# First maxima row in one piece, second stack behind it, b's stores by part

## The reference, cut to what matters

```python
def reference(x, cond, ...):          # x (8, 256, 256), cond (8, 512), all float32
    # layer 0: modulated attention, 16 heads of 16 channels
    xs = layernorm(x * s1)
    q, k = (xs @ Wq.T) * q_dc, (xs @ Wk.T) * k_dc
    v = (xs @ Wv.T) * v_dc * s2
    p = softmax(q @ k.T * 0.25)
    x = x + (p @ v) @ Ww.T * w_dc + (v @ Wu.T) * u_dc
    # layer 1: gated state space, 512 channels, 16 states
    xr, gate = split(x @ W_in.T); xr = xr + cond
    xc = silu(conv4(xr)); xn = layernorm(xc) * g + b
    Bm, Cm, dt = split(xn @ W_xproj.T)
    Ad = 1 - 0.01 * tanh(dt @ W_dt.T + b_dt) * tanh(A_log)
    Bd = Bm * min(norm(xn), 1)
    for t in range(256):              # sequential
        h = clip(h * Ad[t] + Bd[t] x xn[t], -10, 10); y[t] = C[t] . h
    return x + (y + D * xn) * silu(gate) @ W_out.T
```

## Time and profile before

| | |
|---|---|
| median of 3 runs | 540.82 us |
| the profiled execution's own time | 541.88 us |
| its span | 539.0 us |
| TensorE / VectorE / ScalarE / POOL busy | 476.7 / 431.6 / 256.6 / 171.8 us |

### The profile page before, as it was taken

How to read it: one execution, slowest core, us unless ns; L and a number is a source line. 1 busy time by engine, 2 the same in 40 slices (tenths; PEclk the granted TensorE clock), 3 DMA queues, 4 the chain that set the end, 5 groups by cost and what they waited for, 6 DMA issues and landing times.

```text
span 539.0 us, 8625 instructions
## 1 busy us (share of the span) xinstructions
PE 476.7 (88%) x3064; PEld 288.4 (54%) x3084; DVE 431.6 (80%) x751; ACT 256.6 (48%) x512; POOL 171.8 (32%) x195
## 2 busy tenths in 40 slices
PE   6974998999999989888999887689998999999996
PEld 6842765767676656567898453133333333333333
DVE  6795355777857786849998986899999999999994
ACT  3442476767577646779686765343311111111111
POOL 5145303213031100000640100798783334333332
PEclk8695799999999999999999999999999999999999
DMA  8656374553645620100057547676546433333310
GB/s 311 243 176 169 137 176 100 156 142 97 156 99 148 149 77 1 41 19 21 2 198 242 185 150 168 220 265 199 158 136 135 143 116 117 107 104 104 105 36 22
DMA packets 45606, 71.81 MB, mean 133 GB/s; under 512 B 19097, under 2 KB 34073, under 8 KB 42892
## 3 DMA queue, kind: packets, MB, share of 16 engines
q1 hardware_dynamic: 37556, 64.66, 40.7%
q10 hardware_dynamic: 7480, 3.06, 2.3%
q0 software_dynamic: 528, 3.55, 1.7%
HBM read 41.88 MB, written 23.02 MB: 120 GB/s over the span
## 4 chain that ended last, share of the span: by engine, by line
PE 55%; DVE 27%; DMA 7%; ACT 5%; issue 3%; SPq 1%; POOL 1%; ACTq 1%; another core or an unknown queue 0%; DVEq 0%
DVE win L1926 9%; PE bank L1079 7%; PE bank L1537 6%; PE bank L1137 5%; PE bank L1497 5%; DVE z L1926 5%; PE bank L1508 5%; PE bank L1105 5%; PE bank L1122 4%; PE bank L1196 3%; PE bank L1174 3%; DVE acc L1715 3%; DVE lnb_rep L1926 3%; PE bank L1325 2%; DVE zlast L1926 2%
## 5 line engine op out<-in xcount | busy, mean ns | idle before, releaser
L1737 DVE TENSOR_REDUCE mx<-bank 128x2 f32<-128x512 f32 x128 | 82.0, 685 | 58.1 <-PE bank L1105 57.7
L1497 PE MATMUL bank<-xst,bst 128*128 128x512 bf16 x238 | 76.3, 383 | 22.2 <-DVE win L1926 8.9
L763 ACT ACTIVATE ex<-bank 128x512 f32<-128x512 f32 x128 | 70.8, 599 | 40.7 <-PE bank L1122 40.7
L1926 DVE CUSTOM_DVE_ANT_0 win<-win,bank,hi 128x512 f32<-128x512 f32 x96 | 71.8, 748 | 4.0 <-PE bank L1325 0.7
L1508 PE MATMUL bank<-win,cst 128*32 128x512 f32 x256 | 67.3, 605 | 0.2 <-DVE zlast L1926 0.2
L1497 PEld LDWEIGHTS bank<-xst,bst 128*128 128x128 bf16 x256 | 24.6, 97 | 70.4 <-DVE win L1926 27.4
L1105 PE MATMUL bank<-kst,qst 127*128 127x256 bf16 x256 | 48.6, 283 | 8.1 <-DVE mx L1737 7.2
L1122 PE MATMUL bank<-qst,kst 128*128 128x256 bf16 x256 | 46.5, 275 | 9.8 <-DMA qst<-mT 7.1
L1079 PE MATMUL bank<-xnT,w 128*128 128x256 f32 x192 | 49.2, 410 | 1.7 <-ACT xnT L663 0.9
L517 POOL TENSOR_TENSOR qk<-qk,part 128x512 f32<-128x512 f32 x14 | 16.2, 1156 | 101.3 <-ACT part L678 101.3
L621 POOL TENSOR_TENSOR yg<-yT,gateT 128x128 f32<-128x128 f32 x60 | 29.4, 523 | 56.7 <-ACT yT L1012 56.7
(11 more groups left out here) (218 smaller groups left out, 928.1 us busy)
## 6 DMA issues: line engine op xcount, KB each, us to landing
xs_d<-xpart SPq DMA_DIRECT2D x15, 384.0 KB, 4.8
xst<-xs_d SPq DMA_DIRECT2D x15, 384.0 KB
qk_d<-part SPq DMA_DIRECT2D x58, 96.0 KB, 2.4
xn_d<-xc SPq DMA_DIRECT2D x16, 256.0 KB, 4.0
xtk<-xn_d SPq DMA_DIRECT2D x64, 64.0 KB
xst<-xs_d SPq DMA_DIRECT2D x15, 256.0 KB
bd_d<-zeros POOLq DMA_DIRECT2D x1, 3468.0 KB, 13.1
qst<-qk_d SPq DMA_DIRECT2D x7, 384.0 KB, 3.9
```

The source lines that it names most:

```text
L763: nc.scalar.activation(ex[:, n // 4, n % 4, :], bank[6 + n % 2][:, :], ACT.Exp, scale=SCALE)\
L1497: mm(bank[t % 4][:, :], bst[:, slot, t % RS, :], xst[slot][:, t % RS, :], start=True, stop=True)\
L1737: v.tensor_reduce(mx[:, :, STACKED[n]:STACKED[n] + 1], bank[4 + n % 2][:, :].rearrange("p (t k) -> p t k", t=HALVES), AX.X, ALU.max)\
L1926: v._custom_dve(bass.dve_ops.TENSOR_ADD_SAT, out=zst[t % ZR], in0=zst[(t - 1) % ZR], in1=bank[t % 4][:, :], s0=hi[:, t:t + 1], s1=0.0).the ...
```

## The change

Sample 0's row of maxima is made in one piece, like the others: `turn_first_half` and `take_first_half` go, `scores(0, 0, 2)` and the exponentials of its heads move into `sample(0)`. SP stores its half of sample 1's stack, waits for `m_row`, and loads both q and k (six DMAs); ACT stores only. At the hand-over, `split` counts `bsplit` after each part; SP sends pairings 0 to 2 after the first part and 3 after the second, ahead of xn of tile 6; ACT sends x parts of tile 6 and the first rows of tile 7, then pairings 4 and 5. Gates are taken in order 5, 6 and `u_steps(0)` waits for seven. The `store_parts` helper takes the engine as an argument; where nothing else changes in such a line it is left out here.

```diff
@@ SP
                     sp.wait_ge(s["third_ready"], 2)
+                if b == 1:
+                    sp.wait_ge(s["m_row"], 16)
                 if b >= NBUF:
                     sp.wait_ge(s["st_done"], (b - NBUF + 1) * NH)
-                load_stack(sp, b, 0, NH, (f"ld_q{buf}", f"ld_k{buf}"), (0,) if b == 1 else (0, 1))
+                load_stack(sp, b, 0, NH, (f"ld_q{buf}", f"ld_k{buf}"), (0, 1))
...
             sp.wait_ge(s["ld_k1"], 48)
-            sp.wait_ge(s["m_half"], 16)
+            sp.wait_ge(s["m_row"], 16)
...
             store_d(0, "bd_first")
-            store_xn(B - 2)
-            store_parts(B - 2)
-            store_parts(B - 1, 0, FIRST, "xs_first")
             sp.wait_ge(s["bsplit"], 1)
             store_b(sp, 0, range(3), 0, RS, "bd_first")
+            sp.wait_ge(s["bsplit"], 2)
+            store_b(sp, 0, (3,), 0, RS, "bd_first")
+            store_xn(B - 2)
             parts_stored(B - 1)
@@ ACT
-            def take_first_half():
-                act.wait_ge(s["mt_half"], 1)
-                nc.scalar.activation(mT[0:NH // 2, :], bank[3][0:NH // 2, 0:S], ACT.Copy).then_inc(s["mT_half"], 1)
-                act.wait_ge(s["mT_half"], 1)
-                act.dma_start(qstacks[0][M_ROW:P, 0:NH // 2], mT[0:NH // 2, :]).then_inc(s["m_half"], 16)
...
                 act.wait_ge(s["mt_done"], b + 1)
-                if b == 0:
-                    act.wait_ge(s["m_half"], 16)
                 nc.scalar.activation(mT[:, :], bank[3][0:NH, 0:S], ACT.Copy).then_inc(s["mT_ready"], 1)
                 act.wait_ge(s["mT_ready"], b + 1)
-                lo = NH // 2 if b == 0 else 0
-                act.dma_start(qstacks[b % NBUF][M_ROW:P, lo:], mT[lo:, :]).then_inc(s["m_row"], 16)
+                act.dma_start(qstacks[b % NBUF][M_ROW:P], mT[:, :]).then_inc(s["m_row"], 16)
...
-                if b == 0:
-                    exponentials(0, 0, 2)
...
                     take_qk(b + 2, 0, 2)
+                    if b == 0:
+                        exponentials(0, 0, 2)
                     take_qk(b + 2, 1, 3)
...
-            stack_stored(act, 1)
-            load_stack(act, 1, 0, NH, ("ld_q1", "ld_k1"), (1,))
             nc.scalar.activation(minus[:, :], ident[:, :], ACT.Copy, scale=-1.0).then_inc(s["minus_ready"], 1)
-            take_first_half()
...
-                act.wait_ge(s["gate_done"], {5: 14, 6: 13}.get(b, b * 2 + 2))
+                act.wait_ge(s["gate_done"], b * 2 + 2)
...
             third_part(7)
+            store_parts(act, B - 2)
+            store_parts(act, B - 1, 0, FIRST, "xs_first")
             nc.scalar.activation(warm[:, :], ones[:, 0:1], ACT.Silu)
             act.wait_ge(s["zfill"], 16)
-            act.wait_ge(s["bsplit"], 1)
-            store_b(act, 0, range(3, 6), 0, RS, "bd_first")
+            act.wait_ge(s["bsplit"], 3)
+            store_b(act, 0, (4, 5), 0, RS, "bd_first")
             take_gate(4)
             act.wait_ge(s["bd_first"], 16 * 7)
             load_b(act, 0, "ld_bf", 0, FIRST)
+            take_gate(5)
             take_gate(6)
-            take_gate(5)
@@ TensorE
-                if b == 0 and lo == 0:
-                    pe.wait_ge(s["m_half"], 16)
-                if lo == (NH // 2 if b == 0 else 0):
+                if lo == 0:
                     pe.wait_ge(s["m_row"], b * 16 + 16)
...
-                if b >= 1:
-                    scores(b, 0, 2)
+                scores(b, 0, 2)
                 max_scores(b + 1, 0, 2)
...
             max_scores(0, 0, 8)
-            max_scores(0, 8, 10)
-            turn_first_half()
-            max_scores(0, 10, 14)
-            scores(0, 0, 2)
-            max_scores(0, 14, NH)
+            max_scores(0, 8, NH)
...
+            project_gate(5, 2, 4)
             project_gate(6)
-            project_gate(5, 2, 4)
             project_gate(7, 0, 2)
 
-            pe.wait_ge(s["bsplit"], 1)
+            pe.wait_ge(s["bsplit"], 3)
...
-            pe.wait_ge(s["gate_out"], 6)
+            pe.wait_ge(s["gate_out"], 7)
             u_steps(0)
@@ VectorE, split
                 for k in range(2):
-                    own.mark(v.tensor_copy(parts[:, k, 0, :], left))
-                    own.settle()
+                    v.tensor_copy(parts[:, k, 0, :], left).then_inc(s[done], 1)
+                    dve.wait_ge(s[done], k + 1)
```

More of the change, by code:

```diff
@@ L257, in build @@
             rt_out xnb_ready tr_done xnT_ready q_done k_done vt_done v_done q_in k_in vt_in v_in cast0 rem_qk
-            cast1 part_ready pw ld_q0 ld_q1 ld_q2 ld_k0 ld_k1 ld_k2 third_ready m_row stacks_clear pw_first ld_half smax_done maxes mt_done mT_ready mt_half mT_half m_half half_gate wx_ready lnb_made
+            cast1 part_ready pw ld_q0 ld_q1 ld_q2 ld_k0 ld_k1 ld_k2 third_ready m_row stacks_clear pw_first ld_half smax_done maxes mt_done mT_ready half_gate wx_ready lnb_made
             st_done exp_done pv_done pvc_ready att_in att_ready skip_done skip_in mix_done x1_ready wcomp wgain pconst xr_done xr_in tap3_ready gate_done
@@ L310, in load_stack, with store_parts @@
                        .then_inc(s[done[w]], 16)
+        def store_parts(eng, j, lo=0, hi=P, done=None):
+            b, t = FINISHED[j]
+            eng.wait_ge(s["parts_ready"], j + 1)
+            eng.dma_start(xs_d[:, b, t * P + lo:t * P + hi, :].rearrange("k p c -> p k c"),
+                          xpart[lo:hi, j % XRING, :, :]).then_inc(s[done or f"xs_out{j % XRING}"], 16)
         block = ctx.enter_context(nc.Block())
@@ L392, in store_xn @@
                 sp.dma_start(xn_d[t * P:(t + 1) * P, b, :], xc[:, b * HALVES + t, :]).then_inc(s[f"xn_out{t}"], 16)
[L394 to L399, removed]
             def parts_stored(tiles):
@@ L436, in _ @@
                 store_xn(j)
-                store_parts(j)
+                store_parts(sp, j)
             sp.wait_ge(s["zfill"], 16)
@@ L448, in _ @@
             load_x(0, "ld_xf", 0, FIRST)
-            store_parts(B - 1, FIRST, RS, "xs_second")
+            store_parts(sp, B - 1, FIRST, RS, "xs_second")
             store_xn(B - 1)
@@ L454, in _ @@
             load_x(0, "ld_x0", FIRST)
-            store_parts(B - 1, RS, P)
+            store_parts(sp, B - 1, RS, P)
             sp.wait_ge(s["ones_in"], 16)
@@ L1145, in turn_maxima @@
                 pe.wait_ge(s["maxes"], b * NH + NH)
-                if b == 0:
-                    pe.wait_ge(s["mT_half"], 1)
                 for t in range(HALVES):
@@ L1150, in turn_maxima @@
                 ins.then_inc(s["mt_done"], 1)
[L1152 to L1158, removed]
             def project_att(b, bk):
```

## The result

| | before | after |
|---|---|---|
| median of 20 runs each | 541.37 us | 543.64 us |
| ratio, 95% interval | | 1.0053 (1.0036 to 1.0070) |
| profiled execution, its span | 541.88, 539.0 us | 544.2, 542.4 us |

The account below looks back on a forecast made before the run. TensorE's queue was taken to bound the kernel up to about 290 us, VectorE's 256 dependent scan steps from about 342. Third stack +2.8 and hand-over +0.2 gave +3.0 us, forecast 543.8, range 540.0 to 547.0.

Parts of the forecast that it names:

- Part 1: Start of attention: sample 0's row of maxima in one piece, issued at 52.2 us, landing 2.4 us later at 54.6.
- Part 2: Second stack behind the row: 8.7 us on one queue, no cost over two; landed at 63.3, TensorE's maxima +1.2 us.
- Part 3: Third stack, held on SP's queue behind 2.3 MB of layer-1 loads: lands at 86.0 against 83.2, +2.8 us.
- TensorE's own path: TensorE's work up to the third sample's maxima: sample 1 at 78.0, done at 84.0, under the third stack's 86.0.
- 2.2 us for the half clock: Term in TensorE's path through sample 0, added to 63.3 + 12.5 to reach sample 1 at 78.0.
- the +1.2 us: Later start of TensorE's maxima on the second stack, 63.3 instead of 62.09; absorbed, not added to the sum.
- rival B: Sample 0 on TensorE: half clock lasts, it ends 6 us late, third sample at 88, not 86; 545.8 us, chance 0.15.
- Part 4: Hand-over to the scan: +0.2 us, from -0.6 to +0.9; an earlier step 0 is worth nothing because of step 16.
- xn's +0.7: Hand-over: xn of tile 6, 256 KB issued just after the first x store, shares the DMA engines, +0.7 us.
- A: Third stack hidden: its stores slip through the big loads, only the hand-over cost is left; 541.0 us, chance 0.2.
- C: Faster: second stack alone on the DMA engines lands at 59.6, kernel gains 0.9 us; 540.0 us, chance 0.1.
- D: Hand-over grows: x store on ACT's queue lands 1.5 us late behind 640 KB, step 16 too; 545.3 us, chance 0.1.

Follow-up runs that it names:

- e3: Changed kernel, but SP loads the second sample's stack as soon as it is stored, without waiting for the row; 537.68 us, 0.9923 of the kernel before.
- e6: Changed kernel with the second stack loaded without waiting for the row, k's three loads on ACT's queue; 538.09 us, 0.9931 of the kernel before.
- e5: Changed kernel plus unused matmuls in TensorE's two waits, 80 in the first and 30 in the second; 545.12 us, 1.0063 of the kernel before.
- e4: Changed kernel with all four layer-1 loads (2.3 MB) moved behind the second sample's row of maxima; 545.53 us, 1.0081 of the kernel before.
- e7: Changed kernel with the layer-1 loads spread behind the rows of samples 1, 2 and 3; 543.52 us, 1.0034 of the kernel before.
- e9: Changed kernel plus unused matmuls in TensorE's two waits, 80 in the first and 85 in the second; 544.87 us, 1.0071 of the kernel before.
- e1: Kernel before with only the attention half of the change, old hand-over to the scan; 544.24 us, 1.0056 of the kernel before.
- e2: Kernel before with only the hand-over half of the change, attention as before; 540.88 us, 0.9992 of the kernel before.
- e8: Changed kernel, second stack loaded without waiting for the row, xn of tiles 6 and 7 stored behind the x parts; 537.15 us, 0.9918 of before.
- e10: Changed kernel, second stack loaded without waiting for the row, on two queues, xn of tiles 6 and 7 behind the x parts; 538.00 us, 0.9923 of before.

## Why the prediction was right

**Part 1, the row.** Issue and landing came within 0.2 and 0.4 us. I gave the one piece no value of its own; e3 shows that it has one: with the stack loaded early, the kernel takes 537.7 us where before took 541.2 (e3, which has the new hand-over too, worth 0.4 us or nothing), so some 3 to 3.5 us. In e3's profile the half row's landing of 6.34 us behind 1.5 MB is gone (the whole row took 3.0 us), and its first maxima of sample 1 are reduced at R + 16.4 where before they were at R + 20.3.

**Part 2, the stack behind the row, one queue.** 8.7 us forecast and measured; e6 shows no difference between one queue (537.68) and two (538.09).

**Part 3, what waits behind it.** The deciding step held: loads of the third stack at R + 33.7 (33.8 forecast), scores at R + 44.3 (44.1), 3.0 us later than before where the sum had 2.8. TensorE's own path came out as well: at the transposes ahead of the second wait it was at 75.54 (R + 35.75; forecast 78.0, R + 35.8), though its first wait was 5.63 us and not some 4. The 2.2 us for the half clock in that path, and with it the range of 76.8 to 79, no run shows. What the runs show in its place, from the first maxima of sample 1 to those transposes: 13.01 us in e5 (63.61 to 76.62, granted 1.00 throughout) and 14.29 in the kernel after (61.25 to 75.54, granted 0.53 in 62 to 64), so 13.0 at full clock and 1.3 for the low one, where the path had 12.5 and 2.2. (For the maxima of sample 2 my list of signs gave 86, the stack's landing; by the sum it was 86.8.) e3 shows that the wait for the row costs all of it. That it costs by way of the third stack is shown in the profiles: e4 moves the delay to the next stack, e7 removes it; in the runs e7 gives back about 1 us of the 2.9, within the noise, so this step is not shown there. That the +1.2 us and the first low clock are absorbed is seen in TensorE's wait of 2.60 us, and e5 removed the low clock without gain.

**What it missed.** A low clock behind the second wait, 1.7 us (e9). I had placed the cost of the clock only in sample 0. It was rival B's low clock at another place: it came behind a wait, not out of a long burst at low clock. With it the profiles have 4.7 us more at sample 2 and at au of sample 3, where the runs differ by 2.3 (medians) to 2.9 (ratio) in all. This is not the scatter of single executions: counted from R to their last instruction, after and e1 take 502.6 and 502.6 us, before and e2 496.8 and 496.9, so both pairs of profiles put the whole loss at 5.7 to 5.8 us. I take the size from the runs; why they show half of that stays open. That the forecast's 3.0 lies so near them is therefore partly luck: its sum lacks the 1.7.

**A slip in the working.** Rival B's 6 us was too small. The first four matmuls of the scores took 1.04 us at 0.50 and 0.61 at 1.00; by that, 12.5 us at full clock would be some 21 at half (my estimate), 9 more and not 6. It is not in the sum.

**Part 4, the hand-over.** Step 16 kept its distance (23.59 and 23.67; forecast +0.2), though single profiles can't show 0.2 us (e1, with the old hand-over, has 25.01), and e2's interval includes no change. xn's +0.7 was right (3.00 us in e8 and e10 against 3.68 to 3.74). Step 0 was wrong: forecast 0.6 us earlier, it came 0.9 later (10.08 against 9.18; 0.1 to 1.2 over all profiles of either kind), though b's load was issued 0.55 earlier in relation to the x stores (4.09 against 4.64), as forecast. The x load was 0.3 later. Whether step 0 hangs on x or on b's load alone is open: in e8 both came earlier together.

Rivals: A (hidden) fell with TensorE's wait of 2.60 us; C needed a stack in under 6 us and it took 8.7; D fell with e2; B held only as said.

## What to carry to other kernels

Before pricing a load that is held back so that a small urgent transfer lands fast, follow the queue two or three transfers on, to the next consumer. Here holding back the second stack put the third stack's first load 3.0 us later (R + 33.72 against 30.70) and with it the scores of sample 1 (44.31 against 41.31). The small transfer would have found the engines empty anyway, once it was issued in one piece after the big one had landed (e3: busy share 0.00 in 50 to 52, row issued at 52.37). Before moving a block of bulk loads to "later", ask how many us of slack the slot behind it has: in e4 the 2.3 MB in one slot brought a wait of 2.76 us one sample on, in e7, spread over three slots, no such wait came.

## What the runs showed of the hardware that I had not expected

The length of TensorE's wait alone did not decide whether its clock fell. Ahead of the scores of sample 1 the waits and what followed were: 1.76 us (before), 2.07 (e8) and 2.12 (e2), each with the clock at 1.00 after; 1.95 us (e1), with 0.50 in 86 to 88 and 0.65 in 88 to 90; 2.60 us (after), with 0.59 and 0.56 in 84 to 88; 2.76 us (e4, one sample further on), with 0.50 and 0.84 in 108 to 112. The same shows in sample 0, where in the kernels with the early stack TensorE waits for the exponentials before it goes on with the scores: 1.99 us (e3) and 2.02 (e10) with 0.50 in the next 2 us, 2.03 (e6) with 0.60 and 0.55 in 62 to 66, but 2.26 us (e8) with 1.00. What besides the wait decides it is open.

Twelve executions, with the same work on TensorE and VectorE up to R, reached it between 39.8 and 42.6 us, 2.8 us apart, which is as large as the whole effect of the change.
